# A mixture of experts after a graph layer: the experts' work on single tiles of 128 tokens in place of pairs

## The reference

```python
x = x + gnn(layernorm(x), edge_index, W1, b1, W2, b2)
xt = layernorm(layernorm(x))                  # the second one is the ffn's own
top_p, top_idx = top_k(softmax(xt @ Wr + br), 2)
weights = top_p / top_p.sum(-1)
xe = xn * ln_g[e] + ln_b[e]                   # for each expert e
h  = gelu(xe @ W1[e] + b1[e])                 # 256 -> 1024
y  = h @ W2[e] + b2[e]                        # 1024 -> 256
x = x + sum over the token's two experts of weights * y
```

## Time and profile before

| | us |
|---|---|
| median of 3 runs | 2184.47 (2181.71 to 2184.82) |
| profiled execution | 2183.68 |
| its span | 2182.0 |
| PE busy in the span | 1986.6 (91%) |
| DVE, ACT, POOL busy | 1317.4, 819.5, 504.6 |
| experts' products (first and last matmul) | 1555 to 2168 |

### The profile page before, as it was taken

The page is one execution under the profiler, slowest core; times in us unless marked ns, Lnnn a source line. Parts: engine busy times, 40 slices in busy tenths (PEclk is TensorE's granted clock), DMA queues, the critical chain, the costliest instruction groups (busy, mean ns, idle before and its releaser), DMA issues. The chain is left out here.

```text
span 2182.0 us, 42240 instructions
## 1 busy us (share of the span) xinstructions
PE 1986.6 (91%) x14616; PEld 1323.0 (61%) x14617; DVE 1317.4 (60%) x2860; ACT 819.5 (38%) x1837; POOL 504.6 (23%) x636
## 2 busy tenths in 40 slices
PE   1489999999999995899999999994699999999997
PEld 1345555555555552455555555552599999999996
DVE  8876666676766761244444444446766666666664
ACT  4655555555555551011112121211344444444442
POOL 5720000000000001000000000000355566556653
PEclk9999999999999997899999999996799999999998
DMA  7022222222222221556464757554133323332322
GB/s 224 4 119 93 116 119 90 119 107 101 119 90 119 118 90 74 208 174 215 169 220 169 255 193 247 199 211 184 37 51 48 49 47 51 48 49 47 51 47 27
DMA packets 73720, 256.30 MB, mean 117 GB/s; under 512 B 9927, under 2 KB 50312, under 8 KB 59368
## 3 DMA queue, kind: packets, MB, share of 16 engines
q1 hardware_dynamic: 30520, 181.37, 22.0%
q0 software_dynamic: 28944, 60.16, 12.8%
q10 hardware_dynamic: 14112, 12.85, 1.7%
HBM read 139.26 MB, written 115.08 MB: 117 GB/s over the span
## 5 line engine op out<-in xcount | busy, mean ns | idle before, releaser
L662 PE MATMUL mp_o<-rows,m_counts 128*128 128x512 f16 x2401 | 601.0, 381 | 12.8 <-ACT m_counts L762 6.6
L1506 PE MATMUL rp_o<-rows,r_adj 128*128 128x512 f16 x2401 | 551.5, 380 | 34.3 <-DMA r_adj<-adj 34.3
L762 ACT ACTIVATE m_counts<-mp 128x490 f16<-128x490 f32 (+4 forms) x664 | 360.0, 560 | 350.9 <-PE mp L696 345.1
L1506 PEld LDWEIGHTS rp_o<-rows,r_adj 128*128 128x128 f16 x2401 | 235.7, 100 | 283.2 <-issue 38.0
L584 DVE TENSOR_TENSOR m_oh_lane<-lane_b,m_edge_lane 128x1920 f16<-128x1920 bf16 (+1 forms) x209 | 242.0, 1158 | 201.0 <-PE mp L696 199.2
L662 PEld LDWEIGHTS mp_o<-rows,m_counts 128*128 128x128 f16 x2401 | 209.2, 98 | 190.5 <-issue 15.1
L1998 PE MATMUL fp_h<-f_xt,w 128*128 128x256 f16 x2688 | 304.5, 274 | 0.3 <-DVE f_xt L2094 0.3
L2017 PE MATMUL fp_y<-w,f_hh 128*128 x2688 | 302.4, 273 | 0.0
L696 PEld LDWEIGHTS mp<-m_oh_cell,m_oh_lane 128*128 128x128 f16 x3125 | 202.3, 99 | 140.2 <-DVE m_oh_lane L584 19.8
L1998 PEld LDWEIGHTS fp_h<-f_xt,w 128*128 x2688 | 263.9, 98 | 31.4 <-issue 0.6
L2017 PEld LDWEIGHTS fp_y<-w,f_hh 128*128 128x128 f16 x2688 | 263.0, 98 | 30.4
(11 more groups left out here) (210 smaller groups left out, 1649.3 us busy)
## 6 DMA issues: line engine op xcount, KB each, us to landing
adj<-m_counts SPq DMA_DIRECT2D x49, 1568.0 KB, 5.2
r_adj<-adj SPq DMA_DIRECT2D x49, 1568.0 KB, 6.7
r_raw<-in_L_ffn_W_dram POOLq DMA_DIRECT2D x16, 1024.0 KB, 8.4
w_parts<-r_parts POOLq DMA_DIRECT2D x8, 1024.0 KB, 5.8
w<-w_parts SPq DMA_DIRECT2D x4, 2048.0 KB
rows<-in_x_dram SPq DMA_DIRECT2D x7, 896.0 KB, 12.5
r_x<-in_x_dram SPq DMA_DIRECT2D x49, 128.0 KB, 2.0
out_dram<-r_x ACTq DMA_DIRECT2D x49, 128.0 KB, 1.7
```

What stands on the lines that cost most here:

```text
L662: mm = nc.tensor.matmul(ps_o[q], counts[:, q, s, :], k.rows[0][:, s, :], start=i == 0, stop=i == BLOCKS - 1)
L762: last = nc.scalar.activation(counts[:, q, :, lo - b * P:hi - b * P].rearrange("p h (a d) -> p h a d", d=STEP), items[:, :, (lo - first_ds ...
L1506: mm = nc.tensor.matmul(ps_o[q], adj[:, q, s * P:(s + 1) * P], rows[:, s, :], start=s == 0, stop=s == BLOCKS - 1)
```

## The change

Slots are now filled up to a multiple of 128 for each expert, which needs at most 105 tiles (`slot_token` has 106 columns). `tile_expert` holds a number for each tile. A step of the experts' stage handles one tile, and 15 tiles are a turn, so that there are 7 turns, 5 of them in the loop. In a step the first product has 48 weight loads and 48 matmuls of 128 columns in two halves of four blocks, each half in one PSUM bank; the GELU works on 128 x 128; the second product has 24 matmuls. Buffers are rings: 3 for `x32`, `xt` and `hh`, 6 for the PSUM banks and `h32`, 5 for `y`, and 15 for `xg`. `ps_x` and `ps_y` have one bank each.

```diff
-PAIR = 2 * P
-PAIRS = (2 * PAD_NODES + EXPERTS * (PAIR - 1)) // PAIR
-TOKEN_TILES = 2 * PAIRS
-SLOTS = TOKEN_TILES * P
+TILES = (2 * PAD_NODES + EXPERTS * (P - 1)) // P
+TOKEN_TILES = TILES + TILES % 2
...
-M = 4
-PAIR_TURNS = PAIRS // M
-POOL_HOLDS = 3 * M + 3
+M = 15
+TILE_TURNS = TILES // M
+HALVES = 2
+HALF = HB // HALVES
+XR, HR, YR = 3, 6, 5
+POOL_HOLDS = 2 * M + 3
...
-            link(nc.vector.tensor_scalar(cnt[:], cum[:, :, BLOCKS - 1], float(PAIR - 1), None, ALU.add))
+            link(nc.vector.tensor_scalar(cnt[:], cum[:, :, BLOCKS - 1], float(P - 1), None, ALU.add))
...
-            link(nc.vector.tensor_single_scalar(cnt_i[:], cnt_i[:], 8, ALU.arith_shift_right))
+            link(nc.vector.tensor_single_scalar(cnt_i[:], cnt_i[:], 7, ALU.arith_shift_right))
...
+        ps_h = [pb(f"fp_h{b}", [P, BANK], fp32) for b in range(HR)]
+        ps_x = pb("fp_x", [P, D], fp32)
+        ps_y = pb("fp_y", [P, D], fp32)
...
-            def gathers(m):
-                for i in (2 * m, 2 * m + 1):
+            def gather(m):
...
+            def addition(n, m, begun):
+
+                i = m % M
+                pool.wait_ge(y_ready, done(n, m))
+                if begun:
+                    pool.wait_ge(added, n * (16 * M) + 16 * m)
...
+            def transposes(n, m, begun):
+                pe.wait_ge(got[m % M], n * 16 + (32 if m == M else 16))
+                if begun:
+                    pe.wait_ge(x_aff, done(n, m, 1))
+                for c in range(KF):
+                    mm = nc.tensor.transpose(ps_x[:, c * P:(c + 1) * P], xg[:, m % M, c * P:(c + 1) * P], k.ident[:])
+                mm.then_inc(x_t, 1)
...
+            def first_product(n, m, ex, first):
+                pe.wait_ge(x_hi, done(n, m))
+                pe.wait_ge(x_lo, done(n, m))
+                for b in range(HALVES):
+                    if not (first and HALVES * m + b < HR):
+                        pe.wait_ge(act_done, half_done(n, m, b, HR))
+                    for j in range(HALF):
+                        h, i = b * HALF + j, 0
                         for wh, xh in SPLITS:
                             for c in range(KF):
                                 w = k.w[:, bass.ds(ex, 1), 0, wh, c * HIDDEN + h * P:c * HIDDEN + (h + 1) * P][:, 0, :]
-                                mm = nc.tensor.matmul(ps_h[b][:, j * PAIR:(j + 1) * PAIR], w, xt[:, q, xh, c, :],
+                                mm = nc.tensor.matmul(ps_h[ring(m, b)][:, j * P:(j + 1) * P], w, xt[:, m % XR, xh, c, :],
                                                       start=i == 0, stop=i == 5)
...
+            def second_product(n, m, ex, begun):
+                if begun:
+                    pe.wait_ge(y_done, done(n, m, 1))
+                i = 0
+                for b in range(HALVES):
+                    pe.wait_ge(h_hi, half_done(n, m, b))
+                    pe.wait_ge(h_lo, half_done(n, m, b))
+                    for h in range(b * HALF, (b + 1) * HALF):
+                        for wh, xh in SPLITS:
+                            w = k.w[:, bass.ds(ex, 1), 1, wh, h * D:(h + 1) * D][:, 0, :]
+                            mm = nc.tensor.matmul(ps_y[:], hh[:, m % XR, xh, h, :], w, start=i == 0, stop=i == 3 * HB - 1)
+                            i += 1
+                mm.then_inc(down, 1)
...
-                            g = nc.scalar.activation(h32[:, h, :], ps_h[b][:, j * PAIR:(j + 1) * PAIR], ACT.Gelu,
-                                                     bias=k.b1[:, bass.ds(ex[m + 1] * HB + h, 1)], scale=1.0 / SCALE)
+                            g = nc.scalar.activation(h32[:, ring(m, b), j * P:(j + 1) * P], ps_h[ring(m, b)][:, j * P:(j + 1) * P],
+                                                     ACT.Gelu, bias=k.b1[:, bass.ds(ex[m + 1] * HB + h, 1)], scale=1.0 / SCALE)
```

More of the change, by code:

```diff
@@ L1890, in experts @@
         def experts(eng, regs, n):
-            eng.load(regs, k.pair_expert[0:1, bass.ds(n * M, len(regs))])
+            eng.load(regs, k.tile_expert[0:1, bass.ds(n * M, len(regs))])
             return [eng.snap(r, min_val=0, max_val=EXPERTS - 1) for r in regs]
@@ L1897, in every, with done, half_done, ring @@
             turn(0, True, False)
-            with eng.Fori(1, PAIR_TURNS - 1) as n:
+            with eng.Fori(1, TILE_TURNS - 1) as n:
                 turn(n, False, False)
-            turn(PAIR_TURNS - 1, False, True)
-        def tile(n, m, s):
-            return n * (2 * M) + (2 * m + s)
-        def done(n, m, s, ago=0):
-            return n * (2 * M) + (2 * (m - ago) + s + 1)
-        def bank_done(n, m, b, ago=0):
-            return n * (HBANKS * M) + (HBANKS * (m - ago) + b + 1)
+            turn(TILE_TURNS - 1, False, True)
+        def done(n, m, ago=0):
+            return n * M + (m - ago + 1)
+        def half_done(n, m, b, ago=0):
+            return n * (HALVES * M) + (HALVES * m + b - ago + 1)
+        def ring(m, b):
+            return (HALVES * m + b) % HR
         @block.gpsimd
@@ L2028, in turn @@
                         transposes(n, m + 1, True)
-                    first_product(n, m, ex[m + 1], not (first and m == 0))
+                    first_product(n, m, ex[m + 1], first)
                     if not (first and m == 0):
@@ L2079, in split @@
             def split(n, m, ex, begun):
-                q = m % 2
-                for s in range(2):
-                    i = (2 * m + s) % (2 * M)
-                    part = slice(s * P, (s + 1) * P)
-                    src = x32[:, s, :].rearrange("p (c n) -> p c n", c=KF)
-                    dve.wait_ge(got[i], n * 16 + (32 if m == M else 16))
-                    nc.vector.tensor_copy(k.slot_gate[:, bass.ds(tile(n, m, s), 1)],
-                                          xg[:, i, bass.ds(ex + D, 1)]).then_inc(gated, 1)
-                    dve.wait_ge(x_aff, done(n, m, s))
-                    if begun:
-                        dve.wait_ge(up, bank_done(n, m, HBANKS - 1, 2))
-                    nc.vector.tensor_copy(xt[:, q, 0, :, part], src).then_inc(x_hi, 1)
-                    dve.wait_ge(x_hi, done(n, m, s))
-                    nc.vector.tensor_tensor(xt[:, q, 1, :, part], src, xt[:, q, 0, :, part], ALU.subtract).then_inc(x_lo, 1)
@@ L2096, in result @@
-            def result(n, m, ex, begun):
-                for s in range(2):
-                    r = (2 * m + s) % YR
-                    dve.wait_ge(down, done(n, m, s))
-                    if begun:
-                        dve.wait_ge(added, n * (32 * M) + 16 * (2 * m + s + 1 - YR))
-                    nc.vector.scalar_tensor_tensor(y[:, r, :], ps_y[s][:], 1.0 / SCALE,
-                                                   k.b2[:, bass.ds(ex, 1), :][:, 0, :], ALU.mult,
-                                                   ALU.add).then_inc(y_done, 1)
-                    dve.wait_ge(y_done, done(n, m, s))
-                    dve.wait_ge(gated, done(n, m, s))
-                    nc.vector.tensor_scalar(weighted[:, r, :], y[:, r, :], k.slot_gate[:, bass.ds(tile(n, m, s), 1)],
-                                            None, ALU.mult).then_inc(y_ready, 1)
+                q = m % XR
@@ new lines, in split @@
+                src = x32[:, q, :].rearrange("p (c n) -> p c n", c=KF)
+                dve.wait_ge(got[m % M], n * 16 + (32 if m == M else 16))
+                nc.vector.tensor_copy(k.slot_gate[:, bass.ds(n * M + m, 1)],
+                                      xg[:, m % M, bass.ds(ex + D, 1)]).then_inc(gated, 1)
+                dve.wait_ge(x_aff, done(n, m))
+                if begun:
+                    dve.wait_ge(up, half_done(n, m, HALVES - 1, XR * HALVES))
+                nc.vector.tensor_copy(xt[:, q, 0, :, :], src).then_inc(x_hi, 1)
@@ new lines, in split @@
+                dve.wait_ge(x_hi, done(n, m))
+                nc.vector.tensor_tensor(xt[:, q, 1, :, :], src, xt[:, q, 0, :, :], ALU.subtract).then_inc(x_lo, 1)
+            def result(n, m, ex, begun):
+                r = m % YR
+                dve.wait_ge(down, done(n, m))
+                if begun:
+                    dve.wait_ge(added, n * (16 * M) + 16 * (m + 1 - YR))
+                nc.vector.scalar_tensor_tensor(y[:, r, :], ps_y[:], 1.0 / SCALE, k.b2[:, bass.ds(ex, 1), :][:, 0, :],
+                                               ALU.mult, ALU.add).then_inc(y_done, 1)
+                dve.wait_ge(y_done, done(n, m))
+                dve.wait_ge(gated, done(n, m))
+                nc.vector.tensor_scalar(weighted[:, r, :], y[:, r, :], k.slot_gate[:, bass.ds(n * M + m, 1)],
+                                        None, ALU.mult).then_inc(y_ready, 1)
```

177 lines of the change are left out of this document (66 added, 111 removed).

## The result

The changed kernel takes 2339.25 us (median of 4 runs, 2337.12 to 2340.03), the kernel before took 2183.91 on the same chip: a ratio of 1.0711, with a 95% interval of 1.0693 to 1.0730. It is slower by 7%. The forecast of 2294 had the sign and the mechanism, and was 45 us short; 2339 lies inside its range of 2255 to 2350, near the upper end. The profiled execution took 2340.02 us, with a span of 2338.2.

The account below looks back on a forecast made before the run. PE's sequencer, working out weight addresses, was taken as the bound: tiles 715.5 us, heads 12, cold opening 1 make a stage of 728.5 for 612.8; with ends -5.7, 2183.7 + 110 gave 2294 us, range 2255 to 2350.

Parts of the forecast that it names:

- what bounds the tile: Experts' stage: PE's sequencer working out weight addresses, 6.9 us a tile against the array's 5.64; forecast's chance 0.83.
- The price: Time of one address operation on PE's sequencer: 0.128 us, read from stretches giving 128 and 135 ns.
- the turn heads: Start of each loop turn, six within the stage: 2.0 us each, bounds 1.4 and 3.2, 12 us in all.
- The load: Experts' numbers into PE's registers at a turn's head: 27 ns for each register, 0.88 us for 16.
- The jump: PE's branch at a turn's head: 0.21 us, paid in full once the sequencer has no lead.
- The clock: Rival for the stage: gaps between matmuls drop PE to 1.2 GHz, 2680 us in all; chance 0.02.
- the ends: Stage's opening and tail: first product 1.7 us earlier, last results' additions 4 us earlier, together -5.7 us.
- a whole tile earlier: Single ps_x and ps_y: their results are taken that long before being asked for, so one bank each costs nothing.
- The array's pace: Rival: address operations overlap better, the array sets 5.64 us a tile, 2158 us in all; chance 0.08.
- the dearer loads: Rival: weight loads hold back the first product's matmuls, starts an even 81 ns apart; chance 0.03.
- More operations: Rival: PE's sequencer needs over 48 address operations a tile; chance 0.04.
- The deep rings "at nothing": Six PSUM banks for h, three x buffers and five y: they buy slack without gain, other engines lying under 6.9 us.

Follow-up runs that it names:

- run 1: Changed kernel with PE's weight addresses held constant, every tile using the first expert's weights: 2165.51 us, ratio 0.9916.
- run 2: Changed kernel with the first product's split (0,1) addresses worked out anew, 64 address operations a tile: 2556.64 us, ratio 1.1712.
- run 3: Kernel before with addresses worked out anew, 64 or 80 operations a pair in place of 48: 2190.15 us (ratio 0.9999) and 2229.87 us (1.0208).
- run 6: Changed kernel with each turn's expert numbers in their own row of 128 bytes, so register loads are aligned: 2328.33 us, ratio 1.0670.
- run 7: Changed kernel with 5 tiles a turn and rings of 5: numbers aligned to 64 bytes 2321.38 us (1.0626), not aligned 2336.74 us (1.0671).
- run 5: Changed kernel with byte addresses, additions worked out four at a time ahead of their matmuls, 12 operations a tile: 2191.79 us, ratio 1.0032.
- run 9: Changed kernel with additions joined by four, 5 tiles a turn and aligned numbers: 2155.35 us, ratio 0.9868 against the kernel before.
- run 8: Changed kernel with rings of 3 for the halves of h (from 6) and 3 for y (from 5): 2351.65 us, ratio 1.0742.

## Why the prediction was right, and where its sizes were off

**Right: what bounds the tile.** 48 operations, no lead, matmuls of the first product in the operations' pace, ACT, DVE and POOL waiting for PE: runs 1 and 2 show it for the changed kernel, and run 3 the lead that the kernel before has. The price was 0.128 us by two short stretches. In the stage it is 0.124 from one start to the next in the typical case, and 0.132 in the mean, since one in eight or nine takes 0.15 to 0.30. A tile took 6.97 and 6.75 us for 6.9 and 6.6: 75 x 0.07 + 30 x 0.15 = 10 us of the 46 missing in the profiled execution.

**Off: the turn heads.** This is the step that was mis-sized: 2.0 us each, 12 in all, with 3.2 as the upper bound; measured 7.6 in the mean, 45.4 in all. That is 33 of the 46 us. The range held all the same, with the heads far outside their bound, because its upper end allowed 7.3 us for a tile and the tile took 6.97. The 2.0 us are near what run 6 shows for a head with an aligned load and no jump, 2.2 and 2.7. Three parts were missing:

- The load. I took 27 ns for each register from two loads of one and five registers, 0.88 us for sixteen. Aligned, sixteen take 1.11 us, which is near. Five of seven weren't aligned and took 3.8 to 4.1, about 0.25 us for each register. Run 6 and the two of run 7 show that the place alone makes the difference. The Trainium skill (Runtime: NRT & Kernel Launch, Instruction fetch mechanics) gives about 200 ns for each loaded register, and speaks there of loads that the runtime puts in, while these come from SBUF. The loads that were not aligned are near it (0.25), the aligned ones (0.07) are not, so I was wrong to set the rule aside on the evidence of loads that happened to be aligned.
- The jump. I carried 0.21 us over from a loop body of four pairs. With 15 tiles in the body it takes 3.4, with 5 tiles 0.208 (run 7). Between two jumps PE ran 1044 instructions before and 3041 after; 1019 in run 7 and 1175 in run 3 with 80 operations, where the jump took 0.21 us, and 2319 and 2501 in runs 1 and 5, where it took 3.9 to 4.8 us. The Trainium skill (the same section) lets a jump stall when its target isn't among the instructions that the engine holds, and gives PE room for 2048. The runs agree: up to 1175 the jump is cheap, from 2319 on it is dear. I had not applied that rule to the longer body.
- The clock. I had weighed it as a rival for the whole stage and not for the heads. PE stands still for 7.8 us, and the granted clock goes to half. In run 5 a first product at half clock takes 4.78 us for 2.84. In the changed kernel it is 4.69 for 4.00: the sequencer's 4.00 hides a part of what the array loses.

Of the parts run 6 measures the load alone, 11 us, and its heads with and without a jump give the jump with the clock that follows from it: 4 x 4.9, some 20 us. The load, the jump and the clock together are the step from run 5 to run 9: 36 us. How the 4.9 us divide between the jump and the clock no run tells apart; both are only lengths in the trace.

**Off by little: the ends.** The first product starts 2.74 us behind the first gather's transposes (1552.31 to 1555.05) where it started 4.75 behind them, which is the gain of 1.7 and a bit more. It is not seen in the end, because the stage opens 1.74 us later (1552.31 for 1550.57), in a part that the change leaves alone; the other kernels' openings lie between 1550.2 and 1553.1 on two chips, and between 1555.6 and 1557.4 on the third. The tail from the last matmul to the end is 11.6 us where it was 14.0: a gain of 2.4, where I had 4. The part that I worked out came true: from the last matmul to the issue of the last addition it takes 2.5 us where it took 7.0. But POOL's closing DRAIN, which I had left as it was, takes 4.14 us where it took 2.27 (7.17 in the kernels with 5 tiles a turn; why, no run shows). Three rows of it:

```profile
2323.82 2.79 PE L2013 MATMUL fp_y<-w,f_hh 128*128 x24 [0.71 <-DVE f_y L2093]
...
2329.14 1.56 POOL L1936 DMA_INDIRECT out_dram<-f_weighted,f_to  x1 [0.47 <-issue]
...
L1872 POOLq DRAIN  x1: 4144/4144/4144, 2333.2 to 2333.2; - x1
```

The last tile has no first product behind it, so its second product follows the one before directly and waits 0.71 us for the single ps_y. That cover, named as "a whole tile earlier", is gone for one tile only.

**The rivals.** The array's pace and the dearer loads fell with run 1, which has 56 ns for a matmul of 128 columns with its load. The Trainium skill (TensorE: Matmul & The Clock Gate, Back-to-back issue gap) gives about 81 ns; the measurement decides, and it is near the 58 that was worked out from rows 7. More operations fell with the count of 5040. The clock fell at the heads, for 44 us, and not in the stage as a whole. The deep rings "at nothing" hold in the steady state; at the opening run 8 leaves it open.

## What to carry to other kernels

Where an operand's address depends on a register, count the instructions of the engine's own sequencer for each matmul, beside the array's time: here smaller matmuls with the same addresses turned a hidden 48 x 0.13 us for two tiles into the bound for each. Cure it in the addresses: multiply once per loop turn, and work several sums out next to each other, so that they become one instruction (48 down to 12 a tile, 148 us with both). And as long as a sequencer has no lead, everything at a loop's head is paid in full, so keep the body short and the loaded numbers aligned. A short body also made the tile itself 0.2 us cheaper.

## What the runs showed of the hardware that I had not expected

- An address operation costs by being an instruction: a FUSED_REGOPS for one address 124 ns from start to start in the typical case, one addition 113, and four additions joined in one cost so little more that a tile with 12 of them is held by the array alone (5.52 us).
- A load of registers from SBUF: 0.82 us for six and 1.11 for sixteen from a place that is a multiple of 16 bytes from the start of their array, 1.47 and 3.8 to 4.1 from others. Only steps of 20 and 60 bytes were tried against 64 and 128.
- A jump back takes PE 0.21 us with up to 1175 of its instructions in the body, and 3.3 to 4.8 with 2319 to 3283 (the last is run 2). Where between these it becomes dear wasn't tried. Between 1640 and 2110 us the first instruction queue carries 57 packets in the changed kernel, none in the kernel before and in run 7's aligned one, one in run 9.
- A stretch of 11 us in run 8, in which PE got single instructions 0.7 to 2.1 us apart and ACT's table load waited 7.8 us. Its cause is open.
